# Attention block and mixture of experts on one core: residual made under the convolution, constants off GpSimd, chain and expert work interleaved anew

## The reference, cut to what matters

```python
# 1. attention block
qkv = einsum('bchw,oc->bohw', ln_c(x), w_qkv)               # 192 channels; ln_c: over channels, per pixel
dw  = conv5x5_depthwise(qkv, w_dw)
pw  = einsum('bgihw,goi->bgohw', dw, w_pw)                   # 24 groups of 8
# 16 heads of 8: 8 from qkv, 8 from pw
q, k, v = relu(.), relu(.), [. , 1]
kv  = einsum('bhnd,bhne->bhde', k, v)
o   = einsum('bhnd,bhde->bhne', q, kv); o = o[..., :-1] / (o[..., -1:] + 1e-15)
inv = bn_gamma / sqrt(bn_var + 1e-5)
x   = x + (w_proj @ o) * inv + (bn_beta - bn_mean * inv)
# 2. mixture of experts, per pixel t of x
f = ln_t(t); logits = f @ Wg + bg; top 2 of 8, softmax over the two -> w_dense
out = t + sum_e w_dense[e] * (gelu(f @ W1[e] + b1[e]) @ W2[e] + b2[e])
```

## Time and profile before

| | us |
|---|---|
| median of 3 runs | 121.98 (121.91 to 122.46) |
| the profiled execution | 122.06 |
| its span, first to last instruction | 120.3 |
| PE busy | 115.6 |
| DVE busy | 78.6 |
| ACT busy | 70.0 |
| POOL busy | 33.4 |

### The profile page before, as it was taken

One profiled execution on the slowest core, in us unless ns is written; L12 is line 12 of the kernel. 1 busy time (PEld: TensorE's weight loads), 2 busy tenths in 40 slices (PEclk: granted clock), 3 DMA queues, 4 the chain that ended last, 5 costly groups with the idle time before them and its releaser, 6 DMA issues.

```text
span 120.3 us, 3332 instructions
## 1 busy us (share of the span) xinstructions
PE 115.6 (96%) x1282; PEld 85.7 (71%) x1282; DVE 78.6 (65%) x267; ACT 70.0 (58%) x134; POOL 33.4 (28%) x51
## 2 busy tenths in 40 slices
...
GB/s 100 180 182 224 159 8 0 5 5 5 0 0 5 0 3 0 0 5 0 0 3 0 11 173 246 237 46 44 11 242 230 212 220 16 0 0 54 0 0 46
DMA packets 5460, 8.05 MB, mean 67 GB/s; under 512 B 1412, under 2 KB 3908, under 8 KB 5444
## 3 DMA queue, kind: packets, MB, share of 16 engines
...
HBM read 7.24 MB, written 0.59 MB: 65 GB/s over the span
## 4 chain that ended last, share of the span: by engine, by line
PE 83%; DVE 9%; ACT 2%; issue 2%; POOL 1%; POOLq 1%; DVEq 0%
PE PS L996 36%; PE PS L1293 18%; PE PS L1112 13%; PE PS L1071 2%; DVE HEADWISE L898 2%; PE PS L1178 2%; PE PS L1081 2%; PE PS L1008 2%; PE PS L1217 1%; PE PS L1094 1%; PE PS L1203 1%; POOL XP L449 1%; PE PS L1024 1%; DVE XB L717 1%; PE PS L1248 1%
## 5 line engine op out<-in xcount | busy, mean ns | idle before, releaser
L573 ACT ACTIVATE MS<-PS,B 128x512 f32<-128x512 f32 x48 | 29.1, 690 | 7.2 <-PE PS L996 7.0
L996 PE MATMUL PS<-XS,W1H 128*128 128x512 f32 x64 | 26.6, 415 | 0.0
L996 PE MATMUL PS<-XS,W1L 128*128 128x512 f32 x64 | 25.3, 395 | 0.0
L1293 PE MATMUL PS<-MS,W 128*64 128x256 f32 x192 | 22.3, 383 | 0.0
L874 DVE SCALAR_TENSOR_TENSOR WY<-PS,B,HEADWISE 128x256 f32<-128x256 f32 x24 | 10.5, 480 | 14.8 <-PE PS L1293 14.4
L1293 PEld LDWEIGHTS PS<-MS,W 128*64 128x64 f32 x192 | 13.2, 137 | 8.5 <-ACT MS L573 1.5
L996 PEld LDWEIGHTS PS<-XS,W1H 128*128 128x128 f32 x64 | 12.0, 188 | 4.9 <-ACT MS L573 1.0
L1112 PE MATMUL PS<-HEADWISE,BANDS 32*32 32x448 f32 (+2 forms) x480 | 15.3, 564 | 0.0
L449 POOL TENSOR_TENSOR XP<-XP,WY 128x256 f32<-128x256 f32 x4 | 3.2, 808 | 41.1 <-DVE WY L924 40.8
L1112 PEld LDWEIGHTS PS<-HEADWISE,BANDS 32*32 32x32 f32 x480 | 10.3, 103 | 4.5 <-issue 1.5
L996 PEld LDWEIGHTS PS<-XS,W1L 128*128 128x128 f32 x64 | 12.1, 188 | 1.8
...
## 6 DMA issues: line engine op xcount, KB each, us to landing
...
```

Source lines behind the costliest of these rows:

```text
L573: act.activation(hidden(n), PS[:, h_bank(n), :], ACT.Gelu, bias=B1[:, k:k + 1]).then_inc(gelu_done, 1)
L996: return pe.matmul(PS[0:parts, bank, cols[0]:cols[1]], lhsT, rhs, start=start, stop=stop)
L1293: i = pe.matmul(PS[C * b:C * b + C, bank, at:end], W2[:, KC * e + k, :], hidden(KC * (E * s + e) + k)[:, N * b:N * b + N], start=begins an ...
```

## The change

- **Input turned ahead of qkv.** `turn_input` moves from behind the convolution to ahead of `qkv(0)`, and writes banks 4 and 5. The six dummy matmuls ahead of qkv and the one between the two `turn_tokens` go. ACT copies the two banks to XB (`take_input`) between its root and the scaling of qkv. `qkv(2)` and `qkv(3)` wait for these copies, since they write the same banks.
- **Residual under the convolution.** `residual` becomes one addition in place, SBUF to SBUF, and it and `centred_residual` are on DVE's list under the convolution.
- **Batch norm's root.** POOL's two power calls go. ACT takes a square root, and DVE adds a reciprocal and one Newton step to `normalisation`, which moves ahead of `split_low`. `first_v` moves from DVE to ACT, behind `split_high`.
- **Behind the convolution.** `turn_back(3)`, `turn_back_q(2)` and `turn_back_q(3)` go behind `num(0)`. DVE takes `second_heads(0)` and `(2)`, ACT `(1)` and `(3)` (before: DVE 0, ACT 2, 3 and 1).
- **Order.** The calls of the chain, of the experts and of the gates are written in another order on PE, DVE and ACT. `attend` is split into `reciprocals` and `divide`, softmax(0) stands ahead of variance(3), and `gate(1)` and `tokens(1)` stand earlier among the expert layers.

PE, from the last taps of the convolution on. First before, then of the change. L1081 and L1113 are `turn_back`, L1100 is `turn_input`, L1094 and L1124 are `turn_back_q`, L1178 and L1196 are `kv`, L1186 and L1204 are `qt`, L996 and L1018 with KV are `num`, L1203 and L1221 are `attt`.

The diff, cut to its core:

```diff
@@ tables @@
-        WARM_UPS, WARM_UPS_BEFORE_QKV, WARM_UPS_BEFORE_CONV, TILE_BANKS = 3, 6, 4, (7, 5)
-        XT_BANKS = (6, 2)
-        BACK_BANKS, BACK_Q_BANKS = (0, 1, 5, 7), (3, 4, 5, 2)
+        WARM_UPS, WARM_UPS_BEFORE_CONV, TILE_BANKS = 3, 4, (7, 5)
+        XT_BANKS = (4, 5)
+        BACK_BANKS, BACK_Q_BANKS = (7, 0, 5, 4), (3, 1, 2, 3)
@@ gpsimd @@
-            pool.tensor_scalar(INV[:, 0, :], VEC[:, 3 * C:4 * C], BN_EPS, None, ALU.add).then_inc(bn_guarded, 1)
-            pool.tensor_tensor(INV[:, 1, 0:C // 2], ..., HALF[:, 0:C // 2], ALU.pow).then_inc(inv_ready, 1)
-            pool.tensor_tensor(INV[:, 1, C // 2:C], ..., HALF[:, C // 2:C], ALU.pow).then_inc(inv_ready, 1)
@@ scalar @@
+            def take_input(k):
+                act.wait_ge(xt_ready, k + 1)
+                act.activation(XB[:, 0, :, :]...[:, 4 * k:4 * k + 4], PS[:, XT_BANKS[k], :]..., ACT.Copy).then_inc(xb_copied, 1)
             act.activation(DEV1[:, :], VAR1[:, 3, :], ACT.Sqrt, bias=EPS1[:, :]).then_inc(dev1_ready, 1)
+            take_input(0)
+            take_input(1)
             act.wait_ge(r1_ready, 1)
...
+            act.activation(INV[:, 1, :], VEC[:, 3 * C:4 * C], ACT.Sqrt, bias=EPS2[:, :]).then_inc(inv_ready, 1)
             for s in range(PAIRS):
                 first_k(s)
             split_high()
+            for s in range(PAIRS):
+                first_v(s)
@@ vector @@
-            for s in range(PAIRS):
-                first_v(s)
+            normalisation()
+            residual()
...
             take_conv(0)
-            normalisation()
+            centred_residual()
             take_conv(1)
-            second_heads(0)
-            residual()
...
+            second_heads(0)
             second_q(0)
+            second_heads(2)
             second_q(1)
             read_kv(0)
+            read_kv(1)
+            reciprocals(0)
+            divide(0)
             second_q(2)
             second_q(3)
-            centred_residual()
-            read_kv(1)
-            attend(0)
-            read_kv(2)
-            attend(1)
+            reciprocals(1)
+            divide(1)
+            dve.wait_ge(xb_ready, 2)
             centre(0)
             whole(0)
             variance(0)
-            attend(2)
-            read_kv(3)
+            read_kv(2)
+            centre(1)
             scale(0)
@@ tensor @@
             rs()
-            warm_up(WARM_UPS_BEFORE_QKV, TILE_BANKS[1])
+            turn_input()
...
+            pe.wait_ge(xb_copied, 1)
             qkv(2)
+            pe.wait_ge(xb_copied, 2)
             qkv(3)
@@ scalar, chain: the new order @@
+ second_heads(1) place_q(0) place_q(1) relu_qt(0) relu_qt(1) place_q(2) place_q(3) copy_attt(0) copy_attt(1)
+ square_xc(0) relu_qt(2) second_heads(3) square_xc(1) relu_qt(3) copy_xs(0) gelu(0, 0) copy_attt(2) copy_xs(1) ...
+ gelu(0, 6) read_tokens(0) gelu(0, 7) gelu(1, 0) copy_xs(3) gelu(1, 1) ...
@@ tensor, chain: the new order @@
+ turn_back(0..2) turn_back_q(0) turn_back_q(1) kv(0) qt(0) kv(1) qt(1) num(0) turn_back_q(2) turn_back_q(3) turn_back(3)
+ num(1) attt(0) kv(2) proj(0) attt(1) qt(2) proj(1) num(2) qt(3) xt(0) kv(3) first_layer(0, 0) attt(2) num(3)
+ first_layer(0, 1) xt(1) proj(2) gate(0) attt(3) first_layer(0, 2) first_layer(0, 3) proj(3) ...
+ first_layer(1, 0) xt(3) first_layer(1, 1) gate(1) first_layer(1, 2) tokens(1) first_layer(1, 3) first_layer(1, 4)
+ second_layer(0, 4..7) first_layer(1, 5..7) ...
```

260 lines of the change are left out of this document (139 added, 121 removed).

## The result

The changed kernel took a median of 121.54 us (121.29 to 122.14, 21 runs); the kernel before, run beside it, 122.61 (121.91 to 123.18, 21 runs). The ratio is 0.991, with a 95% interval from 0.9894 to 0.9930: faster by 0.9%. The forecast was 121.0 with a range from 120.0 to 122.1. The profiled execution took 121.51, with a span of 119.2 at a mean granted clock of 1.000.

A forecast was written before the change was run, and what follows sets the result against it. PE was taken to bound the kernel. A gain of 1.4 up to `second_layer(0, 0)` less 0.4 at the second gate made 1.0; 122.06 less 1.0, and 0.08 less for the median, gave 121.0, range 120.0 to 122.1.

The forecast's parts named there:

- The start, "no gain": Ahead of the convolution: qkv starts about 0.6 earlier, but the first tap does not, so nothing is gained.
- that chain: Start: R1 at 9.50, DVE and ACT scaling, ACT laying out, DVE's `place_before`, first tap at 15.26; claimed independent of qkv.
- ACT's copies in the hole: Start: two copies of about 0.55 fit between ACT's root and R1, delay at most 0.1, 0.4 as bound.
- Under the convolution, no cost: DVE's added work ends ahead of the drains: `split_low` at 24.3 against 25.63, `centred_residual` at 29.4 against 30.6.
- Behind the convolution: Fewer turns and no `centred_residual` there: `kv(0)` 1.95 earlier, `attt(0)` 2.75 earlier; less 1.07 for `kv(2)`.
- the two waits that I named first: Chain: new PE waits of 0.4 ahead of `proj(1)` and 0.6 ahead of `num(2)`, within new waits of 1.3 together.
- the old waits: Chain: two PE waits go, 0.5 for `copy_attt(3)` and 0.4 for the gate's reader, counted as plus 0.8.
- step by step walk: Chain, over three engines: `second_layer(0, 0)` 1.6 earlier, against 1.2 from the terms; the forecast used 1.4.
- The gate: At `gate(1)`: PE waits for `copy_xs(3)`, on ACT behind `gelu(1, 0)`; minus 0.4.
- (b): Rival, chain: the new waits don't come; gain cut to 1.7 to 2.3 by DVE's bound, 119.7 to 120.3; chance 0.15.
- (c): Rival: waits in series eat the gain, three more of 0.3 leaving 0.1 to 0.6; 121.4 to 121.9; chance 0.2.
- (d): Rival: PE falls back to half pace from 8 to 15 or in the chain's waits; 121.8 to 124.0; chance 0.1.

The follow-up runs named there:

- before's second group: Executions of the kernel before, unchanged, with spans near 121.2 (the shorter group lies near 120.3); the one profiled took 122.82, span 121.1.

## Why the prediction was right, and where it was not

**What bounds the kernel: right.** What PE won or lost behind the convolution went mostly to the end: 0.95 for `centred_residual` put back, 0.7 for eight transposes, 0.35 for the gate's wait.

**The start, "no gain": wrong.** The step that failed is "No step of that chain waits for qkv". From qkv's start to the first scaling 1.04 to 1.05 pass in both profiles of before and in the one with the dummies back (8.58 to 9.63, 9.38 to 10.43, 9.60 to 10.64). In the kernel before qkv thus released the scaling at 9.63, and R1, ready at 9.50, did not. The row of ACT's scaling, which waits for PE, was there to be read. In the profiled execution that was worth only the 0.10 by which the first tap moved. Where PE keeps its half pace through the token transposes it is worth 0.70 (R1 at 9.73, scaling at 10.43), and my one profile was of the other kind. In the changed kernel qkv could release the scaling at 7.93 + 1.05 = 8.98, half a microsecond ahead of R1. That this reserve takes up a late pace is an inference; for it speaks that the spans scatter over 0.9 instead of 1.4 and that none of before's second group is left, while with the dummies back they scatter over 1.4 again. In the medians the dummies cost the kernel before 0.5. The Trainium skill (TensorE: Matmul & The Clock Gate, Part 1: The HAM clock gate) says that the moment at which the pace rises differs from run to run and advises not to fit to it, since it is worth less than 1% of a typical span; the trace agrees in both, with first taps at 15.26 and 16.05, 0.8 of a span of 120. Here that is nearly the size of the whole gain.

**ACT's copies in the hole: right.** 1.06 for the two, 8.42 to 9.48, R1 at 9.49, without the 0.4 kept as a bound.

**Under the convolution, no cost: right.** `split_low` started at 21.24, even earlier than forecast (`normalisation` took 2.63, `residual` 1.22), and `centred_residual` was through at 29.21, 1.29 ahead of the drain.

**Behind the convolution: the mechanism right, some terms off.** `kv(0)` came at 33.05 (33.1), `num(1)` at 38.50 (38.7) and `attt(0)` at 39.49 (39.8): 3.06 earlier where I had 2.75. By the distance of starts, the two waits that I named first cost 0.41 for `copy_attt(1)` (0.4) and 0.47 for `read_kv(2)` (0.6). The third stands at another place: 0.26 ahead of `xt(0)`, for `low(0)`, and none ahead of `first_layer(0, 0)` (0.3). Of the old waits 0.4 went by the same count (0.23 ahead of the `proj` at 54.14 and 0.17 ahead of the first layer at 58.07), where I had 0.8. Another 0.5 less lies in many small differences where one kind of matmul follows another in a new order, which the sum did not have and no run separates. `second_layer(0, 0)` came 1.61 earlier. My step by step walk had said 1.6, the sum of the terms 1.2, and the 1.4 between them was the wrong choice. Why the walk was the better one is not shown; a likely reason is that it sees that a wait shortens the next one. The kernels with `read_kv(2)` moved and with the chain tightened fit this from the other side: taking waits away there gave nothing, because the next one took their place.

**The gate: right.** 0.45 lost (0.4), for the engine and reason given; `combine` was not the bound, with 0.77 of idle time left on DVE, more than the 0.3 that I had worked out.

**The time around the span: not foreseen.** The sum used 1.76 and POOL's powers were costed at "without them nothing moves". That is true of the span; around it the kernel lost 0.5. So the forecast of a gain of 1.0 met the measured 1.07 by luck, through two errors that cancel: 0.5 too little at the start in the medians, 0.5 too much around the span. The chain and the gate are the rest: 120.7 - 0.5 - 119.3 leaves 0.9 in the median spans, against the forecast 1.0. The time itself, 121.0, was 0.54 too low: the forecast started from a profile of before with a span of 120.3, of the shorter group, and three runs around 121.98. Against this group the change wins its 1.0 in the span and gives 0.5 of it back around it, as the profiled pair does (122.06 to 121.51).

**The rivals.** (b), no new waits, and (c), the gain eaten, did not come: PE's waits in the chain went down by 0.3 in all. (d) did not come as I drew it. Qkv takes 2.87 in every start that is shown here, so PE kept its full pace from 8 to 15. The half pace matters earlier, in the kernel before.
